# A decoder block on one core: the order of vector work, row statistics, value products and scores in the mixing stage

## The reference

```
x = x + windowed_attention(layernorm(x))          # 16 heads of 16, window 128, prefix of 16 keys
x = x + cross_attention(layernorm(x), ctx)        # 16 heads, 64 context rows
x = x + ffn(layernorm(x)):
    y = layer_norm(h + mha(h)) * g1 + be1         # h = layernorm(x); 4 heads of 64, attention ACROSS the 8 sequences,
                                                  # for each of the 512 positions by itself
    expert of a row = argmax(y @ Wg.T)            # 8 experts, one per row
    z = layer_norm(y + relu(y @ W1[e] + b1[e]) @ W2[e] + b2[e]) * g2 + be2
```

## Time and profile before

| | |
|---|---|
| median of three runs | 1223.05 us |
| the profiled execution: its own time | 1222.52 us |
| its span | 1220.8 us |
| TensorE busy | 1124.4 us (92%) |
| VectorE busy | 727.6 us (60%) |
| ScalarE busy | 483.6 us (40%) |
| GpSimd busy | 500.4 us (41%) |
| mean granted TensorE clock | 0.983 |

### The profile page before, as it was taken

How to read it: one execution, slowest core, us unless ns; L and a number is a source line. 1 busy time by engine, 2 the same in 40 slices (tenths; PEclk the granted TensorE clock), 3 DMA queues, 4 the chain that set the end, 5 groups by cost and what they waited for, 6 DMA issues and landing times. The chain is left out here.

```text
span 1220.8 us, 29847 instructions
## 1 busy us (share of the span) xinstructions
PE 1124.4 (92%) x10228; PEld 768.5 (63%) x10237; DVE 727.6 (60%) x2056; ACT 483.6 (40%) x863; POOL 500.4 (41%) x721
## 2 busy tenths in 40 slices
PE   8999999999999999999898889888889999999995
PEld 3545455464554644645554455666657999999994
DVE  4555666757766677565725556554565655656553
ACT  5444454445454545445352233322213333333330
POOL 3334425244252443442432222343243566556664
PEclk9999999999999999999999999998979999999998
DMA  7266654644637345364372132348013111111110
GB/s 222 71 186 160 173 155 115 184 111 121 188 105 210 88 143 163 89 192 136 80 203 74 53 105 88 114 136 290 20 41 103 48 46 52 49 53 52 52 44 7
DMA packets 142614, 137.97 MB, mean 113 GB/s; under 512 B 29512, under 2 KB 135886, under 8 KB 142416
## 3 DMA queue, kind: packets, MB, share of 16 engines
q1 hardware_dynamic: 136944, 124.20, 35.4%
q0 software_dynamic: 5280, 12.66, 3.1%
q10 hardware_dynamic: 320, 0.16, 0.1%
HBM read 49.37 MB, written 50.83 MB: 82 GB/s over the span
## 5 line engine op out<-in xcount | busy, mean ns | idle before, releaser
L970 ACT ACTIVATE probs<-ps_ab 128x512 f32<-128x512 f32 (+2 forms) x352 | 174.5, 537 | 92.4 <-PE ps_ab L1292 36.5
L591 POOL TENSOR_SCALAR_AFFINE_SELECT probs<-probs 128x512 f32<-128x512 f32 x128 | 81.9, 640 | 267.0 <-ACT probs L970 263.0
L2810 PE MATMUL ps_ab<-e_yT,e_w_now 128*128 128x128 f32 x1248 | 145.8, 275 | 0.0
L2810 PEld LDWEIGHTS ps_ab<-e_yT,e_w_now 128*128 128x128 f32 x1248 | 142.5, 192 | 0.1
L2821 PE MATMUL ps_c<-keep_w,e_hT 128*128 x624 | 141.0, 379 | 0.0
L2821 PEld LDWEIGHTS ps_c<-keep_w,e_hT 128*128 128x128 f32 x624 | 115.7, 190 | 14.1
L712 DVE CUSTOM_DVE_ANT_0 ps_ab<-ps_ab,mask_qk 128x256 f32<-128x256 f32 x224 | 88.9, 450 | 18.9 <-PE ps_ab L1261 18.8
L706 DVE TENSOR_REDUCE top<-ps_ab 128x2 f32<-128x512 f32 (+1 forms) x112 | 74.1, 683 | 28.4 <-PE ps_ab L1261 27.5
L2745 DVE TENSOR_SCALAR e_hT<-ps_ab,keep_b 128x128 f32<-128x128 f32 x312 | 84.4, 343 | 7.5 <-PE ps_ab L2810 4.6
L1261 PE MATMUL ps_ab<-k_rows,q_rows 96*128 96x256 bf16 (+1 forms) x512 | 84.5, 260 | 4.6 <-DVE top L712 2.7
L1820 ACT ACTIVATE e_w_now<-keep_w 128x1024 f32 x78 | 78.1, 1049 | 22.2 <-issue 12.3
(11 more groups left out here) (236 smaller groups left out, 2120.8 us busy)
## 6 DMA issues: line engine op xcount, KB each, us to landing
sorted_rows<-filler SPq DMA_DIRECT2D x8, 4290.0 KB, 16.9
q_rows<-parts SPq DMA_DIRECT2D x96, 128.0 KB, 2.4
k_rows<-parts SPq DMA_DIRECT2D x96, 128.0 KB, 2.4
q_rows<-q_parts SPq DMA_DIRECT2D x96, 128.0 KB, 2.4
keep_w<-in_e_w SPq DMA_DIRECT2D x16, 512.0 KB
keep_w<-in_e_w SPq DMA_DIRECT2D x8, 1024.0 KB
e_row<-sorted_rows SPq DMA_DIRECT2D x39, 130.0 KB, 2.1
x_in<-in_x SPq DMA_DIRECT2D x8, 512.0 KB, 3.9
```

What stands on the lines that cost most here:

```text
L591: nc.gpsimd.affine_select(own, own, [[0, TILES], [1, P]], ALU.is_ge, keep_zero, base=0, channel_multiplier=-1).then_inc(probs_cut.sem, 1)
L970: nc.scalar.activation(probs[:, user % 2, lo:lo + width], ps_exp[:, f % 2, 0:width], ACT.Exp).then_inc(exp_done.sem, 1)
L2810: mm = nc.tensor.matmul(ps_h[s][:, f // 4, (f % 4) * P:(f % 4 + 1) * P], w1_now[:, s, k, f * P:(f + 1) * P], yT[:, s, k * P:(k + 1) * P], ...
```

## The change

Five moves; no product and no vector operation is added or dropped.

1. VectorE, `iteration`: `normalise` is split into `sum_up` (the wait for the exponential and the sum) and `normalise` (reciprocal, multiplication). `mix(n, 0)` stands between the two, `mix(n, 1)` between `normalise` and `turn`. `ln_statistics(n + 2)` moves from behind `shift_scores` to behind `post_norm_statistics`.
2. VectorE: `slots` of a group moves from the end of its iteration to the next one, behind `shift_scores`.
3. GpSimd, `iteration`: `ln_first(n + 2)` moves from the front to behind `bias` and `post_norm_rstd`.
4. TensorE: `scores(n + 1)` is done in iteration n, between `logits` and `ranks` (before: at the front of iteration n + 1, behind `ranks`).
5. TensorE and ScalarE: v0 comes ahead of yT0 and yT1, v1 right behind them and ahead of logits (before: yT0, yT1, v0, logits, v1, ranks). `MIX_FILLS` follows, and with it the bank of each fill and what it waits for.

```diff
@@ -1759,7 +1759,7 @@
 ROUTE_FILLS = ["out0", "out1", "yT0", "yT1", "logits", "ranks"]
 HALVES_FILLS = ["out0", "out1", "yT0", "logits0", "yT1", "ranks0", "logits1", "ranks1"]
 PROJECT_FILLS = ["xT0", "xT1", "q0", "q1", "k0", "k1", "v0", "v1"]
-MIX_FILLS = ["xT0", "xT1", "out0", "out1", "q0", "q1", "k0", "k1", "yT0", "yT1", "v0", "logits", "v1", "ranks"]
+MIX_FILLS = ["xT0", "xT1", "out0", "out1", "q0", "q1", "k0", "k1", "v0", "yT0", "yT1", "v1", "logits", "ranks"]
 OPENING_FILLS = [f for f in MIX_FILLS if f not in ROUTE_FILLS]
 CLOSING_FILLS = [f for f in MIX_FILLS if f not in PROJECT_FILLS]
 QUADS, QUAD = 4, 32
@@ -2095,18 +2095,18 @@
                             in_=rows[:, (n - 1) % 2, c, :], in_offset=None).then_inc(rows_sent[(n - 1) % 2].sem, 16)
 
                 def iteration(n, ahead=True, more=True):
-                    if more:
-                        ln_first(n + 2)
                     if ahead:
                         for h in range(2):
                             if n > 0:
                                 pool.wait_ge(mixed_ready.sem, mixed_ready.count(n, h + 1))
                             bias(n + 1, h)
-                    if n == 0:
-                        return
-                    for k, own in enumerate(post_norm_parts(n)):
-                        post_norm_rstd(n, k, own)
-                    number_rows(n)
+                    if n > 0:
+                        for k, own in enumerate(post_norm_parts(n)):
+                            post_norm_rstd(n, k, own)
+                    if more:
+                        ln_first(n + 2)
+                    if n > 0:
+                        number_rows(n)
 
                 ln_first(0)
                 position_mask()
@@ -2155,10 +2155,13 @@
                     nc.vector.tensor_tensor(probs[:, :, :, :], ps, least[:, :, :].unsqueeze(3).broadcast_to(wide_blocks),
                                             ALU.add).then_inc(shifted_ready.sem, 1)
 
-                def normalise(n):
+                def sum_up(n):
 
                     dve.wait_ge(exp_done.sem, exp_done.count(n, 1))
                     nc.vector.tensor_reduce(total[:, :, :], probs[:, :, :, :], AX.X, ALU.add).then_inc(total_ready.sem, 1)
+
+                def normalise(n):
+
                     dve.wait_ge(total_ready.sem, total_ready.count(n, 1))
                     nc.vector.reciprocal(scale[:, :, :], total[:, :, :]).then_inc(scale_ready.sem, 1)
                     dve.wait_ge(scale_ready.sem, scale_ready.count(n, 1))
@@ -2244,21 +2247,26 @@
                 def iteration(n, more=True):
                     route = n > 0
                     shift_scores(n)
+                    if n > 1:
+                        slots(n - 1, whole, 0, "ranks")
+                    sum_up(n)
+                    if route:
+                        mix(n, 0)
+                    normalise(n)
+                    if route:
+                        mix(n, 1)
+                    turn(n)
+                    if route:
+                        post_norm_statistics(n, whole)
                     if more:
                         ln_statistics(n + 2)
-                    normalise(n)
-                    turn(n)
                     if route:
-                        mix(n, 0)
-                        mix(n, 1)
-                        post_norm_statistics(n, whole)
                         post_norm_scale(n, whole)
                         post_norm_apply(n, 0, whole)
                     if more:
                         ln_apply(n + 2)
                     if route:
                         choose(n, whole, 0, "logits")
-                        slots(n, whole, 0, "ranks")
 
                 def last_route(n):
                     first_half, second_half = post_norm_parts(n)
@@ -2316,6 +2324,7 @@
                 ln_apply(1)
                 for n in range(NGROUPS):
                     iteration(n, more=n < NGROUPS - 2)
+                slots(NGROUPS - 1, whole, 0, "ranks")
                 last_route(NGROUPS)
                 step_tables()
 
@@ -2371,11 +2380,12 @@
                         queries(n)
                         keys(n)
                     take_heads(n)
+                    if project:
+                        values(n, 0)
                     if route:
                         y_features(n)
                     if project:
-                        for i in range(2):
-                            values(n, i)
+                        values(n, 1)
 
                 act.wait_ge(mask_made.sem, 3)
                 for r in range(QUADS):
@@ -2521,7 +2531,6 @@
 
                 def iteration(n, project=True, route=True):
 
-                    scores(n)
                     if project:
                         features(n)
                     if route:
@@ -2530,14 +2539,16 @@
                         for j in range(4):
                             query_or_key(n, j)
                     heads(n)
+                    if project:
+                        projected_values(n, 0)
                     if route:
                         y_features(n)
                     if project:
-                        projected_values(n, 0)
+                        projected_values(n, 1)
                     if route:
                         logits(n)
                     if project:
-                        projected_values(n, 1)
+                        scores(n + 1)
                     if route:
                         ranks(n)
 
@@ -2550,6 +2561,7 @@
                 for i in range(2):
                     projected_values(-1, i)
                 pe.wait_ge(mask_made.sem, 3 + QUADS)
+                scores(0)
                 iteration(0, route=False)
                 for n in range(1, NGROUPS - 1):
                     iteration(n)
```

## The result

The changed kernel took 1226.83 us (median of 20 runs, 1223.49 to 1230.25) against 1222.88 for the kernel before (20 runs, 1220.19 to 1227.51). The ratio is 1.003, 95% interval 1.002 to 1.0041: a little slower, where 1211 was forecast with a range of 1203 to 1216.

The account below looks back on a forecast made before the run. TensorE was taken as the bound, with only its 3.56 us idle an iteration to win back. Gains of 7.9, 3.5, 0.5 and 0.1 less 0.3 made 11.7 us, so 1211 us, range 1203 to 1216.

Parts of the forecast that it names:

- The unnamed idle in the scores: TensorE's gap within the scores, read as late instructions under GpSimd's row sends: kept at 1.3 us, bounds 0 and 2.6.
- Rival C: Steady iterations: xT1's new 1.1 us idle behind the scores' gap brings the low clock, 4.4 us each; 1229, chance 0.05.
- The queue rule: Instruction blocks come over their own DMA queue, mostly hidden; by it the scores' 1.3 us gap would be 0.
- Steady iteration: Iterations 2 to 4: old TensorE waits go, 1.1 us ahead of xT1 comes; 24.1 us against 25.28, 3.5 gained in three.
- Opening: Iteration 1: x_in lands earlier, `mix` no longer waits, queries and keys run at full clock; gain 7.9 us, bounds 4 and 8.5.
- Iteration 5: TensorE's 2.1 us idle under four back-to-back experts and the low clock come again; 29.3 us against 29.83, gain 0.5.
- Tail: Iteration 7: `slots` takes the place of a wait on VectorE and the chain to y is longer; loss 0.3 us.
- A: Rival: iteration 5 doesn't run dry and gains 5.7 us instead of 0.5; 1206, chance 0.25.
- B: Rival: xT1's new wait costs 1.1 us more in three iterations, or the opening keeps the slow clock (2.8); 1214, chance 0.15.

Follow-up runs that it names:

- sends_early_again: The changed kernel with GpSimd's row sends moved to the front of its iteration, on the fourth chip: 1201.4 us, ratio 0.9827.
- no_sends: The changed kernel without the row sends of iterations 2 to 6: 1202.89 us, ratio 0.988.
- sends_by_sync: The changed kernel with those rows sent by SyncE's ordinary DMAs to a plain block elsewhere in DRAM: 1202.38 us, ratio 0.9872.
- sends_early: The changed kernel with the row sends ahead of all GpSimd does in the iteration, in the first set: 1202.44 us, ratio 0.9876.
- after_again: The changed kernel, unchanged, timed again on the second chip: 1208.97 us, ratio 0.9934.
- stats_back: The changed kernel with the next group's statistics back behind shift and `ln_first` back at GpSimd's front: 1225.58 us, ratio 1.0062.
- best: The changed kernel with sends early, `slots` ahead of shift, both bias additions after the second `mixed`, last expert loads after `heads`: 1203.13 us, ratio 0.9875.
- before_again: The kernel before, unchanged, timed again on the second chip: 1216.13 us, ratio 0.9996.
- before_sends_early: The kernel before with the row sends ahead of all GpSimd does in the iteration, on the fourth chip: 1214.12 us, ratio 0.993.

## Why the prediction was wrong, by its own steps

- **The unnamed idle in the scores.** This is the step that failed: "The sends would begin at about T+19 now and still cover the scores. I read the gap as instructions that arrive late, and keep 1.3 us; bounds 0 and 2.6". The times were right to a tenth (sends at T+19.3, scores at T+21.2 in iteration 2); the price was not. The rows at hand warned of it: the sends from 793.63 to 798.5 and the scores from 798.10 overlap by half a microsecond before, and by the forecast's own times the overlap after would be whole (sends T+19 to T+24, scores T+21.2 to T+22.8). The 1.3 was the price of a glancing meeting. The whole one cost 3.5 us in the scores (4.8 against 1.3), and then the low clock in the next output, transposes and keys: 27.3 us an iteration against 22.3 with the sends elsewhere. The forecast's 24.1, 24.1, 24.1, 29.3, 23.9 are 125.5; they took 137.4. On the milder chips the whole meeting costs 1.2 us, near the 1.3 kept, but there the kernel before pays nothing for its edge, so the gain is short by this term all the same.
- **Rival C (0.05)** had the right outcome, the right mechanism (a clock that falls in the steady iterations) and nearly the right price (1229). It was put at xT1's wait behind an unchanged scores' gap. On the first occasion that is the wrong place: the clock fell within the scores' stops, ahead of the wait. `sends_early_again` keeps the wait at 0.90 and 0.91 us five times and has the full clock each time; over the four kernels of this order without the collision (`no_sends`, `sends_by_sync`, `sends_early`, `sends_early_again`) the clock fell in 3 of 20 iterations with that wait, twice ahead of it. Where the wait grows, to 1.54 in `after_again` and 2.7 in `stats_back`, falls do come behind it.
- **The queue rule.** That blocks of instructions arrive unnoticed ("mostly hidden", the Trainium skill, "Runtime: NRT & Kernel Launch", section "Instruction fetch mechanics") isn't borne out by the stops with nothing named: 2 us of them in 128 products under sends, 1.25 us in iteration 5. That late instructions are what these stops are is still an inference. Shown is that the row of stops goes with GpSimd's indirect sends over small products; single stops come without sends too, 0.32 us in `no_sends`, 1.66 in `best`, and 1.04 in an output of `before_again`, while weights move at 384 GB/s.
- **Steady iteration: right.** The waits of 1.34, 0.25 and 0.82 us went, the new one of 0.9 (1.1 forecast) came, and without the collision the period is 22.3 to 22.5 against 22.8 forecast ahead of the gap.
- **Opening: right.** 21.71 against 21.75 in iteration 1, no wait for x_in, 7.27 us of queries and keys at full clock.
- **Iteration 5: place right, size off.** The idle came (1.25 us, not 2.08) at nearly the same place: six products of v0 behind `heads`, where five transposes were before. The low clock in it was the collision's: with the sends early it takes 23.90 with an idle of 1.32 still in it. The sum for this iteration also held no gap in the scores at all, which took 4.6 us (850.79 to 855.39). The near hit of 28.66 on 29.3 is therefore luck: 4.4 of low clock behind the idle were forecast, and scores and their clock came. The idle doesn't always bring the low clock either: in `before_again` and `before_sends_early` it is 2.06 and 2.00 us at this place, the clock stays at 1.00, and the iteration takes 25.25 and 25.05 us. `best` shows that the back-to-back experts cause the idle at this place, since it goes from there when they are paced.
- **Tail:** 0.5 us lost, 0.3 forecast.
- **The chances:** forecast, A and B add up to 0.90, so 0.91 for faster was a slip; nothing hangs on it.

What stays open is why the same program loses on two occasions (stops of 0.2 to 1.2 us) and gains on two others (2.5 to 2.6 us from the first score product to the least value in the iterations compared, stops of at most 0.3): 1.003 and 1.0038 against 0.9934 and 0.9964. Before differs in the same sense, 1222.6 to 1222.9 against 1216.1 to 1217.4. With the sends early the changed kernel takes 1202.4 and 1201.4 on a chip of either kind, so, as far as these runs show, the chips differ in the price of the collision alone. That the sends' place is the cause is shown on one chip with both orders; why sends stop small products, and how much of the loss is the clock, is not. What in the chip sets this price no run shows.

## What to carry to other kernels

When two engines' work is moved, write down the stretch of each on one time axis, before and after, and ask which pairs newly overlap; a cost that was seen once at the edge of an overlap is not the price of the whole overlap, which here was nearly three times as much. Put GpSimd's indirect sends under long products rather than under a hundred tiny ones: on the fourth chip that alone is worth 25.9 us in one order and 8.5 in the other, on the milder chips some 7 to 10 in the changed order (1209.0 and 1212.7 against 1202.4), and it gives the fastest kernel measured, 0.9827 (0.9814 to 0.984) of before. A reordering whose worth depends on such a meeting should be measured on more than one chip before its sign is believed.

## What the runs showed of the hardware beyond that

**A multiplication that takes 1.7 us instead of 0.69.** In iteration 1 of the kernel after, and of all that share its order but `best`, VectorE's multiplication runs beside GpSimd's bias addition. VectorE and GpSimd there:

```profile
728.29 1.70 DVE L2168 TENSOR_TENSOR m_probs<-m_probs,m_scale 128x512 f32<-128x512 f32 x1
```

```profile
728.17 1.27 POOL L2070 TENSOR_TENSOR m_xnb<-m_xn,m_b_o 128x512 f32<-128x512 f32 x1 [11.77 <-DVE m_mixed L2184]
```

In `sends_early_again` from iteration 2 on GpSimd is sending at that time, and the same multiplication takes 0.69:

```profile
772.16 0.69 DVE L2166 TENSOR_TENSOR m_probs<-m_probs,m_scale 128x512 f32<-128x512 f32 x1
```

The 1.0 us more is near the 1.15 that was left of the addition when the multiplication began, 728.29 to 729.44. In `best`, where the addition waits, it takes 0.69 in iteration 1 too. The Trainium skill, "SBUF — State Buffer", section "🔬 SBUF: two separate sides", says that VectorE and GpSimd lock each other out there for operations of this kind; by that rule the multiplication waits until the addition is through, and the trace agrees within 0.15 us.

**The first products of the stage.** Queries and keys of group 0 took 7.13 us in the kernel before and 8.74 after. The profiled executions of before's order all have the shorter time to the first least value (18.96 to 19.18 us after the stage's start, 4 of 4); those of the changed kernel itself have 20.63, 20.63, 20.80 and 19.17. TensorE's granted clock from 696 to 698 us was 0.51 after and 1.00 before. Of the 14 profiled executions in the new order, variants included, 8 have the long form (8.7 to 8.8 us) and 6 the short one. Nothing that the change edits runs in that stretch, and no cause was found.
